# A gated graph network with inputs laid out by nodes and by features ahead of the launch

## The reference

```python
h = x
for _ in range(3):
    a_in = einsum('nm,bmd->bnd', adj, h)          # a_out is the same, as both matrices are adj
    av = concatenate([a_in, a_out], axis=-1)
    z = sigmoid(av @ w3_w.T + w3_b + h @ u3_w.T + u3_b)
    r = sigmoid(av @ w4_w.T + w4_b + h @ u3_w.T + u3_b)
    hv = tanh(av @ w5_w.T + w5_b + (r * h) @ u5_w.T + u5_b)
    h = (1 - z) * h + z * hv
out = layernorm(x + h, axis=-1)
```

## Time and profile before

| | us |
|---|---|
| median of three runs (769.85 to 770.3) | 770.13 |
| the profiled execution | 770.7 |
| its span, first to last instruction | 768.7 |
| TensorE busy | 752.5 (98%) |
| VectorE busy | 612.0 (80%) |
| ScalarE busy | 438.8 (57%) |
| GpSimd busy | 67.3 (9%) |

### The profile page before, as it was taken

The page is one execution under the profiler, slowest core; times in us unless marked ns, Lnnn a source line. Parts: engine busy times, 40 slices in busy tenths (PEclk is TensorE's granted clock), DMA queues, the critical chain, the costliest instruction groups (busy, mean ns, idle before and its releaser), DMA issues.

```text
span 768.7 us, 10991 instructions
## 1 busy us (share of the span) xinstructions
PE 752.5 (98%) x3722; PEld 637.8 (83%) x3722; DVE 612.0 (80%) x969; ACT 438.8 (57%) x745; POOL 67.3 (9%) x91
## 2 busy tenths in 40 slices
PE   7999999999999999999999999999999999999994
PEld 6888888888888888888888888888888888888883
DVE  3787688868997778787988777888789867888785
ACT  3565555556766555555666655555567655555564
POOL 0000012100000011110010001120000000211003
PEclk9999999999999999999999999999999999999997
DMA  7811642122265372222156336222225632221223
GB/s 188 144 29 28 104 76 38 30 37 40 39 130 123 66 131 42 32 39 40 29 114 118 71 76 120 38 37 33 37 39 117 138 64 38 32 32 32 43 36 112
DMA packets 285234, 52.15 MB, mean 68 GB/s; under 512 B 267386, under 2 KB 284420, under 8 KB 285188
## 3 DMA queue, kind: packets, MB, share of 16 engines
q1 hardware_dynamic: 284916, 51.24, 35.8%
q10 hardware_dynamic: 272, 0.26, 0.1%
HBM read 18.95 MB, written 8.39 MB: 36 GB/s over the span
## 4 chain that ended last, share of the span: by engine, by line
PE 95%; DVE 2%; DMA 1%; issue 1%; ACT 1%; POOL 0%; ACTq 0%; SPq 0%; POOLq 0%; DVEq 0%
PE ps_a L353 11%; PE ps_uz L328 11%; PE ps_uz L329 11%; PE ps_uz L330 11%; PE ps_v L328 11%; PE ps_v L330 11%; PE ps_v L329 11%; PE ps_r L328 6%; PE ps_r L330 6%; PE ps_r L329 6%; DMA x_in<-in_x 1%; PE ps_uz L426 0%; DVE dz L647 0%; DVE hT L657 0%; DVE stats L757 0%
## 5 line engine op out<-in xcount | busy, mean ns | idle before, releaser
L519 ACT ACTIVATE ps_v<-ps_v,bias 128x512 f32<-128x512 f32 x96 | 63.6, 662 | 73.0 <-PE ps_v L330 73.0
L642 DVE TENSOR_TENSOR dz<-ps_v,hT 128x512 f32<-128x512 f32 x64 | 44.2, 691 | 76.4 <-ACT ps_v L519 76.4
L543 ACT ACTIVATE ps_r<-ps_r,bias 128x512 f32<-128x512 f32 x96 | 63.5, 662 | 71.1 <-DVE ps_r L663 70.2
L514 ACT COPY u_sb<-ps_uz 128x512 f32<-128x512 f32 x96 | 56.4, 587 | 73.5 <-PE ps_uz L330 73.5
L501 ACT CAST aT_hi<-ps_a 128x512 fp32r<-128x512 f32 x96 | 56.1, 586 | 65.5 <-PE ps_a L353 65.4
L328 PE MATMUL ps_uz<-hT_hi,wt_lo 128*128 128x512 f32 x192 | 79.1, 412 | 0.0
L552 ACT CAST rh_hi<-rh 128x512 fp32r<-128x512 f32 x96 | 59.6, 621 | 28.2 <-DVE rh L668 28.2
L329 PE MATMUL ps_uz<-hT_lo,wt_hi 128*128 128x512 f32 x192 | 75.1, 391 | 0.0
L330 PE MATMUL ps_uz<-hT_hi,wt_hi 128*128 128x512 f32 x192 | 75.0, 391 | 0.0
L328 PE MATMUL ps_uz<-aT_hi,wt_lo 128*128 128x512 f32 x192 | 74.9, 390 | 0.0
L328 PE MATMUL ps_r<-aT_hi,wt_lo 128*128 128x512 f32 x192 | 74.9, 390 | 0.0
(11 more groups left out here) (84 smaller groups left out, 1564.8 us busy)
## 6 DMA issues: line engine op xcount, KB each, us to landing
hn<-hb SPq DMA_DIRECT2D x736, 32.0 KB, 2.0
x_in<-in_x SPq DMA_DIRECT2D x16, 512.0 KB, 5.0
x_blk<-in_x SPq DMA_DIRECT2D x64, 128.0 KB, 3.7
out<-y SPq DMA_DIRECT2D x15, 512.0 KB, 3.0
wide<-in_L_gnn_w_w SPq DMA_DIRECT2D x3, 512.0 KB, 4.2
out<-y SPq DMA_DIRECT2D x2, 256.0 KB, 2.1
square<-in_L_gnn_u_w ACTq DMA_DIRECT2D x1, 256.0 KB, 3.3
square<-in_L_gnn_u_w SPq DMA_DIRECT2D x1, 256.0 KB, 4.6
```

The costliest lines, as they stand in the source:

```text
L514: nc.scalar.copy(u_sb[:, oc, :], ps_uz[:, oc, :]).then_inc(u_copied, 1)
L519: nc.scalar.activation(ps_v[:, oc, :], ps_v[:, oc, :], ACT.Tanh, bias=bias[:, BV, oc:oc + 1]).then_inc(v_ready, 1)
L543: nc.scalar.activation(ps_r[:, oc, :], ps_r[:, oc, :], ACT.Sigmoid, bias=bias[:, BR, oc:oc + 1]).then_inc(r_ready, 1)
L642: nc.vector.tensor_tensor(dz[:, c, :], ps_v[:, c, :], h_of(j)[:, c, :], ALU.subtract).then_inc(d_ready, 1)
```

## The change

The inputs are laid out before the launch: x by nodes (`x_rows`: node, graph, feature, so a partition's piece of a load is 4 KB and partitions are 64 KB apart) and by features (`x_cols`: feature, group, chunk, row; 2 KB pieces), adjacency and weights transposed, the five biases as one array. The output is written by nodes too, and turned back afterwards. The transposes of adjacency, weights, biases and x on TensorE and VectorE are taken out, with their copies from PSUM, and the 128-byte loads. `xT` is loaded straight, for rounds after the first behind the moves of frame 8 + q. The filler transposes go from 10 and 26 to 24 and 8. The order of the loads, of ScalarE's first splits and of U5 and W5 changes.

```diff
+        def xT_loads(i, q):
+            return DMA * (i + (C if q == 0 else 1))
-        PREPARED = (U3, W4, W3, U5, W5)
+        PREPARED = (U3, W4, W3, W5, U5)
+        SUMMED = (W4, W3, W5)
+        def weight(k):
+            return square[k - U3] if k in (U3, U5) else wsum[k]
...
-            def load_blocks(i, q):
-                for f in range(QUADS):
-                    sp.dma_start(x_blk[q % 2][f * BLK:(f + 1) * BLK, :, :, :],
-                                 x_blocks[f, :, :, bass.ds((SLOTS * i + q) * NBLK, NBLK), :])\
-                      .then_inc(blocks_loaded[q % 2], DMA)
+            def load_cols(i, q, c=slice(0, C)):
+                sp.dma_start(xT[q][:, c, :], x_cols[:, bass.ds(SLOTS * i + q, 1), c, :].rearrange("p g c r -> p (g c) r")).then_inc(xT_loaded[q], DMA)
...
-                sp.wait_ge(xT_ready[oq], oi + 1)
-                load_blocks(i, q)
                 sp.wait_ge(a_ready, 2 * frames(oi, oq))
                 load_rows(i, q)
...
                 if carry or j > 0:
-                    move(*frame_before(i, j))
+                    bi, bj = frame_before(i, j)
+                    move(bi, bj)
+                    if refill and bj >= FR - SLOTS:
+                        load_cols(bi + 1, bj % SLOTS)
...
+            sp.dma_start(adjT[:, :], adj_t).then_inc(adjT_loaded, DMA)
             load_rows(0, 0)
-            load_blocks(0, 0)
+            for c in range(C):
+                load_cols(0, 0, slice(c, c + 1))
+            load_wide(W4)
+            load_wide(W3)
+            load_wide(W5)
             load_rows(0, 1)
+            load_cols(0, 1)
+            sp.dma_start(square[1][:, :, :], u5_t).then_inc(w_loaded[U5], DMA)
+            load_cols(0, 2)
+            load_cols(0, 3)
...
                 pe.wait_ge(ident_ready, 1)
-                keep_warm(10)
-                pe.wait_ge(adj_loaded, DMA)
-                nc.tensor.transpose(adj_bank, adj_in[:, :], ident[:, :]).then_inc(adj_transposed, 1)
-                transpose_weight(U3)
-                pe.wait_ge(adjT_ready, 1)
+                keep_warm(24)
+                pe.wait_ge(adjT_loaded, DMA)
                 aggregate(0, 0)
-                keep_warm(26)
+                keep_warm(8)
                 weight_ready(U3)
-                u_product(0, 0, between=transpose_weight)
-                pe.wait_ge(bias_loaded, 5 * DMA)
-                nc.tensor.transpose(bias_bank, bias_rows[:, :],
-                                    ident[0:5 * C, 0:5 * C]).then_inc(bias_transposed, 1)
-                transpose_weight(W3)
-                transpose_weight(U5)
+                u_product(0, 0)
                 weight_ready(W4)
-                pe.wait_ge(bias_copied, 1)
                 gate_r(0, 0)
-                transpose_weight(W5)
                 weight_ready(W3)
                 gate_z(0, 0)
                 weight_ready(W5)
                 value(0, 0, False)
+                first_half(0, 1)
                 weight_ready(U5)
-                first_half(0, 1)
                 candidate(0, 0)
...
             weight_high(U3)
+            h_high(0, 0, 0)
+            h_high(0, 0, 1)
             for hf in range(2):
                 a_high(0, 0, hf)
-            for c in range(C):
-                h_high(0, 0, c)
...
-                if following and following[1] < SLOTS and (carry or j > 0):
-                    transpose_x(*following)
...
             weight_low(U3)
-            transpose_x(0, 0)
             for c in range(C):
                 h_low(0, 0, c)
...
+            weight_low(W5)
             weight_low(U5)
-            weight_low(W5)
-            transpose_x(0, 1)
```

More of the change, by code:

```diff
@@ L56, with build @@
 EPS = 1e-5
-def build(nc, x, adj, w3_w, w3_b, u3_w, u3_b, w4_w, w4_b, w5_w, w5_b, u5_w, u5_b, out):
-    B, N, D = x.shape
+def build(nc, x_rows, x_cols, adj_t, w3_t, w4_t, w5_t, u3_t, u5_t, biases, out_rows):
+    N, B, D = x_rows.shape
     ROWS = 512
@@ L92, in build @@
         neg_half = sb("neg_half", [P, GB])
-        wide = [sb(f"wide{k}", [P, C, 2 * D]) for k in range(3)]
+        wide = [sb(f"wide{k}", [P, 2, C, D]) for k in range(3)]
         square = [sb(f"square{k}", [P, C, D]) for k in range(2)]
@@ L271, in store, with frame @@
                              y[q % 2][:, :, :]).then_inc(stored[q % 2], DMA)
-            def frame(i, j, carry):
+            def frame(i, j, carry, refill):
                 if j < 2:
@@ L306, in _ @@
                 for j in range(EARLY, FR):
-                    frame(i - 1, j, True)
+                    frame(i - 1, j, True, True)
                 for j in range(EARLY):
-                    frame(i, j, True)
+                    frame(i, j, True, True)
             last = ROUNDS - 1
             for j in range(EARLY, FR - 1):
-                frame(last, j, True)
+                frame(last, j, True, False)
             for q in range(SLOTS - 1):
@@ L355, in aggregate, with u_product @@
                     done.then_inc(a_ready, 1)
-            def u_product(i, j, between=None):
+            def u_product(i, j):
                 pe.wait_ge(hT_hi_ready, C * frames(i, j))
@@ L403, in candidate @@
                     dense(ps_v, U5, oc, rh_hi, rh_lo, False, True).then_inc(vpre_ready, 1)
[L405 to L417, removed]
             def weight_ready(k):
@@ L556, in weight_high @@
             def weight_high(k):
[L557 to L562, removed]
+                if k in SUMMED:
+                    act.wait_ge(wsum_ready, SUMMED.index(k) + 1)
+                else:
+                    act.wait_ge(w_loaded[k], DMA)
+                nc.scalar.copy(wt_hi[k][:, :, :], weight(k)[:, :, :]).then_inc(wt_hi_ready, 1)
+            act.dma_start(square[0][:, :, :], u3_t).then_inc(w_loaded[U3], DMA)
+            act.dma_start(bias_in[:, :, :], biases).then_inc(bias_loaded, DMA)
             act.wait_ge(neg_half_ready, 1)
             nc.scalar.activation(table_probe[:, :], neg_half[:, :], ACT.Sigmoid)
-            act.wait_ge(adj_transposed, 1)
-            nc.scalar.copy(adjT[:, :], adj_bank).then_inc(adjT_ready, 1)
             weight_high(U3)
+            h_high(0, 0, 0)
+            h_high(0, 0, 1)
             for hf in range(2):
                 a_high(0, 0, hf)
-            for c in range(C):
-                h_high(0, 0, c)
             weight_high(W4)
             copy_u(0, 0)
-            act.wait_ge(bias_transposed, 1)
-            nc.scalar.copy(bias_in[:, :, :], bias_bank.rearrange("p (n c) -> p n c", c=C)).then_inc(bias_copied, 1)
             weight_high(W3)
+            weight_high(W5)
             weight_high(U5)
-            weight_high(W5)
             act.wait_ge(bias_ready, 3)
@@ L720, in weight_low @@
                 dve.wait_ge(wt_hi_ready, PREPARED.index(k) + 1)
[L721 to L722 removed]
+                nc.vector.tensor_tensor(wt_lo[k][:, :, :], weight(k)[:, :, :], f32(wt_hi[k][:, :, :]),
+                                        ALU.subtract).then_inc(wt_lo_ready, 1)
             weight_low(U3)
[L726 removed]
             for c in range(C):
@@ L733, in _ @@
             sum_halves(W3)
-            dve.wait_ge(bias_copied, 1)
+            dve.wait_ge(bias_loaded, DMA)
             for b, (l, r) in ((BZ, (0, 1)), (BR, (2, 1)), (BV, (3, 4))):
@@ L826, with w, features_first @@
     from concourse.bass_utils import run_bass_kernel_spmd
+    x, adj = np.asarray(inputs["x"]), np.asarray(inputs["adj"])
+    B, N, D = x.shape
+    C, GB = D // P, 4
+    def w(name):
+        return np.asarray(inputs[f"L0_gnn_{name}_w"])
+    def features_first(a, parts):
+        return a.T.reshape(parts, C, P, D).transpose(2, 0, 1, 3)
+    bias_names = ("w3", "u3", "w4", "w5", "u5")
+    laid = {
+        "x_rows": x.transpose(1, 0, 2),
+        "x_cols": x.reshape(B // GB, GB * N, C, P).transpose(3, 0, 2, 1),
+        "adj_t": adj.T,
+        "w3_t": features_first(w("w3"), 2),
+        "w4_t": features_first(w("w4"), 2),
+        "w5_t": features_first(w("w5"), 2),
+        "u3_t": features_first(w("u3"), 1)[:, 0],
+        "u5_t": features_first(w("u5"), 1)[:, 0],
+        "biases": np.stack([np.asarray(inputs[f"L0_gnn_{k}_b"]).reshape(C, P) for k in bias_names]).transpose(2, 0, 1),
+    }
     nc = bacc.Bacc("TRN2", target_bir_lowering=False, num_devices=1)
     arrays, args = {}, []
-    for name in _INS:
-        a = np.ascontiguousarray(inputs[name])
+    for name, a in laid.items():
+        a = np.ascontiguousarray(a)
         arrays[f"in_{name}"] = a
         args.append(nc.dram_tensor(f"in_{name}", a.shape, mybir.dt.from_np(a.dtype), kind="ExternalInput").ap())
-    args.append(nc.dram_tensor("out", inputs["x"].shape, F32, kind="ExternalOutput").ap())
+    args.append(nc.dram_tensor("out", (N, B, D), F32, kind="ExternalOutput").ap())
     build(nc, *args)
     result = run_bass_kernel_spmd(nc, [arrays], core_ids=[0])
-    return result.results[0]["out"]
+    return np.ascontiguousarray(np.asarray(result.results[0]["out"]).transpose(1, 0, 2))
```

48 lines of the change are left out of this document (9 added, 39 removed).

## The result

The changed kernel takes 763.56 us (763.27 to 763.82, 4 runs) against 770.05 (769.85 to 770.3, 4 runs): ratio 0.9915, 95% interval 0.9898 to 0.9933. The forecast was 762.0, in a range of 760.8 to 764.8. The gain is 6.5 us; the prediction's sum had 8.3. The profiled execution took 763.27 us with a span (first to last instruction) of 760.5.

What follows compares the result with a forecast made beforehand. TensorE was taken to bound the frames, so only the front could shrink: 5.58 (U3 product sooner) plus 2.69 (transposes and wait) gave 8.3 us off, 761.8 against the median, 762.0 with W4's thin margin; range 760.8 to 764.8.

Steps and rivals of the forecast that it cites:

- The bound and the frames: Steady frames: TensorE, busy 98% of the span, never waits there, so a frame stays at 15.40 us.
- rival (c): The 48 frames get shorter too, as SBUF and queues are freer: 6 us more, 756; chance 0.03.
- t0 from 14.58 to 9.0: 5.58: Front of the kernel: the first U3 product starts at 9.0 us instead of 14.58, saving 5.58 us.
- t0: Start time of the first U3 product on TensorE; 14.58 us before, 9.0 forecast, ends 8.5 and 11.9.
- Transposes and W3's wait, 2.69: Between first U3 product and frame (0,1): weight and bias transposes and the wait for W3's sum go, 2.69 us.
- The tail, taken as nothing: After 743 us only the stores change, to 4 KB pieces: 0 to 0.4 us, counted as nothing.
- rival (a): Late front, by x_in at 7.94 us or a slow clock: 763.6 to 764.7 us; chance 0.20.
- Hiding of the splits: Front: splitting weights on VectorE and ScalarE stays hidden behind TensorE's work, W4 with only 0.2 us to spare.
- U5's due time (t0 + 7.2): Front: U5 must land by 16.2 us or TensorE waits for z in frame (0,1); landing forecast at 15.0.
- The DMA estimate: First loads: at 347 GB/s x by nodes lands at 5.2 us, x by features at 6.7, U5 at 15.0.
- its sign, under 4.5 us: Front: x_in landing under 4.5 us from issue would show the forecast right.
- Rival (d): Round boundaries: xT refills land late if a landing takes over 12.7 us; 784 at 20 us a landing; chance 0.02.

Runs made afterwards that it cites:

- the second profile's chain: Waits in a second profile of the unaltered changed kernel, from its rerun beside the partial changes; that rerun measured 763.49 us (before 769.57).
- second profile of the kernel before: The kernel before, unchanged, profiled once more: 770.2 us, span 767.2.
- the first runs: The changed kernel again and three partial changes, on one chip; the changed kernel took 763.49 us against 769.57 before.
- the last experiment: The changed kernel with U5's load queued behind the loads of x by features for slots 2 and 3: 763.41 us.
- The first two partial runs: Against the kernel before: only weights, adjacency and biases laid out ahead, 769.67 us; only x and output re-laid, fillers as before, 767.22 us.

## Why the prediction was right, and where it missed 1.8 us

- **The bound and the frames: right.** 15.40 a frame with and without the transposes of x; rival (c) fell.
- **The term mis-sized: "t0 from 14.58 to 9.0: 5.58".** Its end held within a microsecond: 9.45, and 9.77 in the second profile's chain (frame (0,1) at 20.67). Its start did not. In the second profile of the kernel before the product starts at 12.81, and the spans of its other executions (median 767.2) agree with that one and not with 768.7. So the term is 3.0 to 3.4. I took one execution for the kernel, though its 6.62 us for x_in was the longest landing of x_in in that trace and rows 6 had 3.0 for as many bytes. The wait named was wrong with it: in the second profile, and in both of the kernel with the weights alone, the product waits last not for x_in but for the blocks of x and their transpose, and it is these that loading x by features takes away.
- **Transposes and W3's wait, 2.69: right.** 13.59 less 11.00 is 2.59; from the second profile (26.66 - 12.81 = 13.85) it is 2.85.
- **The tail, taken as nothing: 0.5 won.** From frame (0,1) to ScalarE's last activation lie 736.9 us in both profiles of before and 736.5 in both after. All of that 0.4 is in one place: VectorE stands idle 0.55 us ahead of `meanvar` before and 0.15 after, 725 us into the chain. The kernel with x alone has 0.15 too and the one with the weights alone 0.55, so it comes with the part on x; why is open. The last stores, now of 4 KB pieces, give the other 0.1.
- **The sum, made again** from the second profile of before: 12.81 to 9.45 is 3.36, transposes 2.85, tail 0.5, together 6.7, which is what the spans show (767.2 to 760.5). The time outside the span takes some of it back (medians 2.55 and 3.06). Measured 6.5, and 6.1 on the chip of the first runs.
- **The range held in part by luck.** Its upper end was meant for a late front of the changed kernel (rival (a), 763.6 to 764.7), and 763.56 lies next to it; but that kernel's front was not late. It was the old kernel's that had been taken for slower than it is.
- **Hiding of the splits: right.** W4's remainder was ready with 0.7 us to spare (0.2 forecast), and with the product 1.5 us earlier it became a wait of 0.60. U5's due time (t0 + 7.2) is borne out by the last experiment: t0 was 8.9 there, so U5 was due at 16.1; it landed at 16.48 and the first wait appeared, 0.17 us.
- **The DMA estimate: too low in rate, too early in the first landings.** Traffic ran at 393 to 426 GB/s from 6 to 13 us where I took 347, and U5 landed at 14.3, not 15.0. But x by features landed at 7.17, not 6.7, and x_in took 4.4 and 4.2 us from issue in the two profiles of the changed kernel, so it was in at 5.7 and 5.5, not 5.2 (its sign, under 4.5 us, held). The pitch of 64 KB did no harm that shows: 350 GB/s from 4 to 5 us, 426 from 9 to 10, and the kernel with x by nodes and the output at the old pitch was not faster (764.13). The page of the Trainium skill that was weighed there (DMA: Bandwidth & Descriptors, section "Latency and other measured facts") gives its 207 GB/s for a pitch of 512 KiB, and no run here has such a pitch.
- **The clock: right in kind.** TensorE started at 1.52, and by the spacing of its matmuls full speed came back at some moment between 5 and 7.5 us, another one in each profile. A late clock, rival (a), was priced at t0 = 11.9 with all fillers ahead of the product; the kernel without fillers has its whole aggregation at half clock and t0 = 9.61.
- **Rival (d) was a real danger, and under-priced.** Its 12.7 us in hand are 12.85 in the trace. With the refill one frame later the kernel takes 75 us more than the changed one. The prediction's arithmetic had one wait at each of three boundaries; the run shows four at each, 52.3 us in all, and 25.7 us more of TensorE's busy time at the lower clock, which the arithmetic left out.

What each part is worth depends on the fillers. Alone, the weights give 0.0 and x 2.35, while both together give 6.1, on the same chip: the parts do not add up. With fillers that fit (32 and 36 for the weights, 10 and 10 for x), the weights alone give 2.4 and x alone 3.8. These add up to 6.2, about the 6.1 to 6.5 of the whole. The first two partial runs taken alone would have called the weights worthless.

## What to carry to other kernels

Profile the start of a kernel more than once before its time is used as a term: the steady part of this one repeated within 0.01 us, while the start of its first product differed by 1.8 us between two profiles. When parts are taken back one by one, refit whatever was tuned around them (here the fillers), or a part looks worth nothing because TensorE meets it with a slow clock. For a prefetch queued behind a frame's DMAs, ask how many frames of slack it has: here it had less than one, and queueing it one frame later cost 75 us. What the chain of waits shows as last may still be worth nothing when taken out, if another path ends just behind it: here the fillers.

## What the runs showed of the hardware

- The record gives the clock as 1.00 in the first microseconds, while the filler transposes come 0.21 to 0.23 us apart, twice what they take later (0.11); there the rate can be read from the spacing alone.
- After 3.15 us without work the clock was at 0.50 for the next product (weights alone); after 3.06 us in the kernel with the late refill it was at 1.00.
- With four DMAs of 128-byte pieces queued behind it, x_in landed 6.6 and 6.7 us after its issue in two profiles (the first of before, weights alone) and 4.3 in two others; in the nine profiles without them it took 4.0 to 4.8. So they may hold up what was issued ahead of them, but not in every execution; what decides it is open. SyncE took 6.1 us over the four issues in the two slow cases and 4.2 in the others.
- Beside GpSimd sums of 128 x 512 tiles, a VectorE remainder that reads SBUF twice took 1.6 times as long (1.12 us against 0.68) and one bias sum 1.24 us in place of 0.15; the two `aT_lo` remainders, which read PSUM, took 1.28 as elsewhere.
- The time outside the span is 1.7 to 3.1 us for the same program; the kernel without fillers had 1.8 in each of four executions. The cause stays open.
